# Perceiver kernel on one Trainium2 core: minima and token mixing on GpSimd, paired tokens in dilated attention, output by halves of the heads, and the last unit turned on TensorE

## The reference, cut to what matters

```python
# L0 token mixing (attn): Xn = layernorm(X) * gamma + beta
Q, K, V = split(Xn @ W_in + b_in)
K, V = rotary(K), rotary(V)
A = sum_over_tokens(K / |K| * V / |V|)
Y = ((0.5 * A + 0.5)[:, None, :] * Q) @ W_out + b_out
# L1 cross attention: 16 heads of 16, 4096 keys (both contexts), 8-bit steps
attn = softmax(q @ k.T)            # q, k rounded by head, v by column
attn = round(attn / s) * s         # s = max(attn) / 255
x += concat(attn @ v) @ Wp + bp
# L1 dilated attention: segments of 64 tokens, even heads take the even
# tokens, odd heads the odd ones; q = k = v = the gathered tokens
out = softmax(g @ g.T * hd ** -0.5) @ g
```

## Time and profile before

| | us |
|---|---|
| runs | 771.82, 774.67, 775.24 |
| profiled execution: its own time | 774.18 |
| its span, first to last instruction | 772.9 |
| PE busy | 673.9 (87%) |
| DVE busy | 587.5 (76%) |
| ACT busy | 373.3 (48%) |
| POOL busy | 124.6 (16%) |
| mean granted TensorE clock | 0.949 |

### The profile page before, as it was taken

How to read it: one execution, slowest core, us unless ns; L and a number is a source line. 1 busy time by engine, 2 the same in 40 slices (tenths; PEclk the granted TensorE clock), 3 DMA queues, 4 the chain that set the end, 5 groups by cost and what they waited for, 6 DMA issues and landing times. The chain is left out here.

```text
span 772.9 us, 12776 instructions
## 1 busy us (share of the span) xinstructions
PE 673.9 (87%) x4880; PEld 427.3 (55%) x4880; DVE 587.5 (76%) x1143; ACT 373.3 (48%) x581; POOL 124.6 (16%) x138
## 2 busy tenths in 40 slices
PE   5899999999999998997998999877897878778543
PEld 4456766666676675675665767633553434334231
DVE  3797867957866879787684787299989999999135
ACT  4453433343343343344332544137678987769411
POOL 3374234333433201000000000001000010000010
PEclk9999999999999998999999999989999999989755
DMA  9478967656665677964685747467788999779800
GB/s 300 103 144 157 189 130 124 130 117 127 119 124 123 144 142 195 206 138 91 137 177 112 150 100 143 86 180 152 146 146 145 202 173 147 152 129 165 151 1 7
DMA packets 334940, 108.24 MB, mean 140 GB/s; under 512 B 301464, under 2 KB 332320, under 8 KB 334624
## 3 DMA queue, kind: packets, MB, share of 16 engines
q1 hardware_dynamic: 334880, 107.43, 69.3%
HBM read 32.16 MB, written 0.26 MB: 42 GB/s over the span
## 5 line engine op out<-in xcount | busy, mean ns | idle before, releaser
L800 PE MATMUL psum<-c_nat,eT 128*128 128x256 f16 x1536 | 191.3, 276 | 0.0
L1455 ACT ACTIVATE cT<-psum,bias,q_scale 128x1024 f16<-128x1024 f32 x128 | 153.7, 1203 | 43.5 <-PE psum L1401 37.1
L1401 PE MATMUL psum<-kT,v_space 128*128 128x512 f16 x512 | 144.5, 390 | 34.1 <-DVE tops L1482 32.4
L774 PE MATMUL psum<-cT,qk 128*128 128x512 f16 x768 | 171.0, 379 | 1.2 <-ACT cT L711 1.1
L800 PEld LDWEIGHTS psum<-c_nat,eT 128*128 128x128 f16 x1536 | 152.3, 99 | 26.9 <-issue 0.6
L1482 DVE TENSOR_REDUCE tops<-psum 128x1 f32<-128x512 f32 x256 | 160.0, 682 | 1.6 <-PE psum L1401 1.4
L774 PEld LDWEIGHTS psum<-cT,qk 128*128 128x128 f16 x768 | 74.9, 98 | 86.0 <-ACT cT L711 1.3
L1401 PEld LDWEIGHTS psum<-kT,v_space 128*128 128x128 f16 x512 | 45.2, 98 | 108.1 <-DVE tops L1482 82.6
L924 DVE TENSOR_REDUCE neg_max<-psum 128x1 f32<-128x2048 f32 x32 | 73.3, 2290 | 31.3 <-PE psum L774 31.2
L912 DVE TENSOR_TENSOR e_lo<-e_all,e_hi 128x2048 f16<-128x2048 f32 x32 | 76.8, 2401 | 0.5 <-DMA eT<-e_lo 0.5
L438 POOL TENSOR_TENSOR rstd<-rstd,minus_half 128x1 f32<-128x1 f32 x12 | 9.5, 792 | 375.1 <-DVE rstd L433 375.1
(11 more groups left out here) (219 smaller groups left out, 740.9 us busy)
## 6 DMA issues: line engine op xcount, KB each, us to landing
wq_h<-in_L_xattn_Wq SPq DMA_DIRECT2D x32, 128.0 KB, 2.3
wk_h<-in_wkT SPq DMA_DIRECT2D x32, 128.0 KB, 2.2
wv_h<-in_L_xattn_Wv SPq DMA_DIRECT2D x32, 128.0 KB, 2.3
wo_h<-in_L_xattn_Wo SPq DMA_DIRECT2D x32, 128.0 KB, 2.2
mx_land<-in_mx_weights SPq DMA_DIRECT2D x8, 384.0 KB, 3.5
v_space<-in_ctx SPq DMA_DIRECT2D x4, 512.0 KB, 7.1
cT<-in_ctx SPq DMA_DIRECT2D x2, 1024.0 KB, 10.8
c_nat<-in_expert_wT SPq DMA_DIRECT2D x2, 1024.0 KB, 6.6
```

The costliest lines, as they stand in the source:

```text
L774: ins = pe.matmul(s_ps[:, n * 512:(n + 1) * 512], c.qk[:, u % 2, q_part, k, :], m.cT[:, b, c_part, 4 * n:4 * n + 4, k, :], start=(k, q_par ...
L800: ins = pe.matmul(u_ps, c.eT[:, v % 2, e_part, j, :], m.c_nat[:, v // H0, c_part, j, :], start=(j, e_part, c_part) == (0, 0, 0), stop=(j, ...
L1401: return pe.matmul(ps, m.qT[:, b, group, r, :], m.kT[:, group, at:at + BLK], start=True, stop=True)
L1455: act.activation(x.y[:, u % 2, q * CHUNK:(q + 1) * CHUNK], m.bank(3 + 2 * (q % 2), 2), ACT.Exp, bias=x.bias[:, u:u + 1], scale=m.q_scale[: ...
```

## The change

**Second stage.** `dve_attention` keeps the maxima alone. The smallest of eight goes to GpSimd (`pool_attention`): four `tensor_scalar` of one column, each as soon as two or three more maxima are there, the last with the factor q_scale, and a fifth for the constant. GpSimd's other work is woven into the same stream by slots.

**Token mixing.** For both batches, gamma, beta, the additions to x, the rotation, the product and the norms go from `dve_mix` to `pool_mix`. The two passes for 0.5·A + 0.5 and Q become one, and a factor 0.5 goes to ScalarE's copy. The slots of batch 0 stay; for batch 1 one is added behind `turn` and one behind `unit`.

**Output.** By halves of the heads. Heads 0 to 7 of batch 0 are woven in behind the queries of batch 1 (slots 43 to 46), those of batch 1 at slots 106 to 109. The values' scale no longer multiplies the result: GpSimd multiplies it into Wp's rows once (`wp1_scaled`), so two diagonals, one product and one copy of the first stage go.

**Dilated attention.** TensorE adds the tokens of a pair (product with the table `pair`); VectorE sets the groups apart from PSUM; scores, maximum, subtraction and exponential go by halves; two heads' exponentials are turned in one transpose of 128 columns, and four products of 64 columns take the place of eight of 32. Five tables come in one DMA.

**Last unit.** Its two DMA transposes go. TensorE turns eight blocks of 512 by products with the identity, VectorE copies seven, ScalarE one.

The core of the diff:

```diff
-MIX_WOVEN = "xT+plus qkv0 qkv1 qkv2 turn squares product unit a yT out"
+MIX_WOVEN = "xT+plus qkv0 qkv1 qkv2 turn turning squares product unit united a yT out"
-OUT_WOVEN = "gather yT out"
-DIL_WOVEN = "apply xT own s0 s1 nat t0+den t1 t2 t3 pv"
+OUT_WOVEN = ("gather0 yT0 out0", "gather1 yT1 out1")
+DIL_WOVEN = "apply xT own nat s0 s1+exp0 t0+exp1 t1+den pv"
...
+def pool_mix(pool, m, x, s, b, at):
...
+    pool.tensor_tensor(m_b, m_b, w["gamma"], ALU.mult).then_inc(sem, 1)
+    pool.wait_ge(sem, MIX_POOL["gamma"])
+    pool.tensor_tensor(m_b, m_b, w["beta"], ALU.add).then_inc(sem, 1)
...
+def pool_attention(pool, m, x, s, side):
...
+        for k in range(NB // 2):
+            top = [x.tops[:, u, n:n + 1] for n in range(2 * k + (k > 0), min(2 * k + 3, NB))]
+            side.upto(NC * u + k - ahead)
+            pool.wait_ge(s["q_max"], min(NB * u + 2 * k + 3, NB * (u + 1)))
+            if k > 0:
+                pool.wait_ge(s["q_steps"], NC * u + k)
+            if k == 0:
+                ins = pool.tensor_scalar(least, top[0], top[1], top[2], ALU.min, ALU.min)
+            elif k < NB // 2 - 1:
+                ins = pool.tensor_scalar(least, least, top[0], top[1], ALU.min, ALU.min)
+            else:
+                ins = pool.tensor_scalar(least, least, top[0], m.q_scale[:, b, h:h + 1], ALU.min, ALU.mult)
+            ins.then_inc(s["q_steps"], 1)
+        pool.wait_ge(s["q_steps"], NC * (u + 1))
+        pool.tensor_scalar(x.bias[:, u:u + 1], least, float(np.log(255.0 / N_UP)), None, ALU.add).then_inc(s["q_bias"], 1)
...
+    def turn(n):
...
+        pe.wait_ge(s["q_exp"], NC * (UNITS - 1) + n * BLK // CHUNK + 1)
+        if n >= 3:
+            pe.wait_ge(s["q_back_dve"], n - 2)
+        if n == 0:
+            pe.wait_ge(s["q_max"], NB * UNITS)
...
+            if u >= UNITS and q < 2:
+                for n in range(NB // 4 * (2 * (u - UNITS) + q), NB // 4 * (2 * (u - UNITS) + q + 1)):
+                    turn(n)
             if u > 1 and q < 2:
                 attend(u - 2, q)
...
+    for n in range(NB - 1):
+        dve.wait_ge(s["q_back"], n + 1)
...
+        back(dve.tensor_copy, x, m, n).then_inc(s["q_back_dve"], 1)
...
+def pe_output(pe, m, x, a, s, b, half, room, at):
+    sem, cols = s[f"at_pe{b}"], half_of(half, D)
+    yield at[f"gather{half}"]
+    yield from pe_leave(pe, room, at[f"gather{half}"], s[f"at_dve{b}"], AT_DVE[f"over_sum{half}"])
...
+    for k in range(KD):
+        ins = pe.matmul(room[1][:, k * OWN:(k + 1) * OWN], x.mine[:, k * P:(k + 1) * P], a.pair[:, 0:OWN], start=True,
+                        stop=True)
...
+    for n in range(PAIRS // 2):
+        pe.wait_ge(s[f"dil_act{b}"], DIL_ACT["t1" if n >= PAIRS // 4 else "t0"])
+        ins = pe.matmul(room[7][:, n * DIL * DW:(n + 1) * DIL * DW], x.scT[:, n, :], flat(x.nat[:, n]), start=True,
+                        stop=True)
```

More of the change, by code:

```diff
@@ L89 @@
 CONSTANTS = steps("zeros ones minus_half ident ident16 ident_fp16")
-V_SCALE_PE = steps("turned spread inverse")
-V_SCALE_DVE = steps("top clamp over diag0 diag1 idiag0 idiag1 scale inverse")
+V_SCALE_PE = steps("turned inverse")
+V_SCALE_DVE = steps("top clamp over diag0 diag1 inverse")
 MIX_PE = steps("xT q k v a yT out")
 MIX_ACT = steps("xT k_norm v_norm yT")
-MIX_DVE = steps("gamma beta plus_norm plus_bias q k v turn0 turn1 cos rotated product norms unit a y added")
+MIX_DVE = steps("q k v y added")
+MIX_POOL = steps("gamma beta plus_norm plus_bias turn0 turn1 cos rotated product norms root unit")
 EX_PE = steps("xT gate prod0 prod1 prod2 prod3 prod4 prod5 prod6 prod7 coefT bias")
@@ L100 @@
 QU_DVE = steps("biased scaled amax clamp inverse over up both0 both1")
[L101 to L106, removed]
+AT_PE = steps("yT0 out0 yT1 out1")
+AT_ACT = steps("yT0 yT1")
+AT_DVE = steps("total0 over_total0 over_sum0 added0 total1 over_total1 over_sum1 added1")
+DIL_PE = steps("xT own nat s0 s1 t0 t1 pv")
+DIL_ACT = steps("xT nat0 nat1 exp0 exp1 t0 t1")
+DIL_DVE = steps("parity apart0 apart1 s0 top0 less0 s1 top1 less1 den inv share over added")
 FF_PE = steps("aT g0 u0 g1 u1 g2 u2 g3 u3 mT0 mT1 out")
@@ L343, in __init__ @@
         self.bp1 = sb("bp1", [P, D])
-        self.mask = sb("mask", [P, OWN])
-        self.row_mask = sb("row_mask", [P, DIL])
+        self.sets = sb("sets", [P, SETS])
+        self.mask = self.sets[:, 0:OWN]
+        self.pair = self.sets[:, OWN:OWN + P]
+        self.row_mask = self.sets[:, OWN + P:OWN + P + DIL]
+        self.blocks = self.sets[:, OWN + P + DIL:SETS - DIL]
+        self.halves = self.sets[:, SETS - DIL:SETS]
 class AttentionTiles:
@@ L841, in pe_cross @@
         if u == H0 + 1:
[L842 to L845, removed]
+            pe.wait_ge(s["v_scale_dve"], V_SCALE_DVE["diag1"])
+            pe.matmul(kv_ps[:, 0:D], m.ones[:, :], g.diagonals[:, :], start=True, stop=True).then_inc(
+                s["v_scale_pe"], 1)
         if 0 <= v < UNITS:
@@ L1049, in dve_value_scales @@
     dve.wait_ge(sem, V_SCALE_DVE["over"])
[L1050 to L1053, removed]
+    for k in range(KD):
+        dve.tensor_scalar(g.diagonals[:, k * P:(k + 1) * P], m.ident[:, :], g.inverse[:, k:k + 1], 1.0 / N_UP,
+                          ALU.mult, ALU.mult).then_inc(sem, 1)
     dve.wait_ge(s["v_scale_pe"], V_SCALE_PE["inverse"])
-    dve.tensor_copy(m.v_scale[:, :], ps[:, D:2 * D]).then_inc(sem, 1)
     dve.wait_ge(s["scores"], H0)
@@ L1485, in dve_attention @@
[L1485 to L1496 removed]
+        least = x.least[:, u:u + 1]
```

380 lines of the change are left out of this document (208 added, 172 removed).

## The result

| | before | after |
|---|---|---|
| median of 4 runs, us | 774.94 (771.82 to 775.24) | 750.55 (746.82 to 751.36) |
| ratio, 95% interval | | 0.9685 (0.9644 to 0.9725) |
| profiled execution / its span, us | 774.18 / 772.9 | 750.32 / 749.0 |

The account below looks back on a forecast made before the run. TensorE was taken to bound the first attention, VectorE the second, before a serial tail. From 774.2 us, minus 12.0 (second attention), minus 8.0 (tail), plus 1.5 (first stage) gave 755.7 us, range 746 to 767.

Parts of the forecast that it names:

- Parts 1 to 3: Second attention: minimum, bias and batch 1's mixing leave VectorE, other work comes; 15.5 us off VectorE, 12.0 off the time.
- Part 4: Serial tail after the last exponential: turning, output and dilated attention gain 8.0 us together, from 5 to 10.
- (a): Tail, last exponential to division: TensorE turns the last unit instead of two DMA transposes; gain 1.6 us, 0 to 3.5.
- (b): Tail, output by the last eight heads: v_scale step goes, transposes, product and division are halved; gain 2.1 us.
- (c): Tail, dilated attention: new order with earlier start and eight product instructions instead of sixteen; gain 4.3 us, 3 to 5.5.
- Part 5: First stage: one product fewer, but batch 0's mixing on GpSimd delays TensorE; +1.5 us in all, -1 to +5.
- The term of the scales: First stage, line 844: one of two TensorE products goes and the wait before them shortens; -0.8 us.
- The term of beta: First stage: gamma and beta on GpSimd each wait for a VectorE step, so beta reaches TensorE later; +2.2 us.
- A: Second attention: DMA transposes or TensorE's hand-overs take over as bound, leaving 4 of 12 us; 763.7 us, chance 0.18.
- C: Second attention: GpSimd's chain of minima becomes the bound, ScalarE's first exponential waiting for the bias; 792 us, chance 0.04.
- D: Whole kernel: minima net 0, tail gives 5 us, TensorE's first-stage stalls cost 5; 774 us, chance 0.03.
- B: Whole kernel: second attention's relief comes whole at 16 us, tail gives 9, first stage 0; 749 us, chance 0.12.

Follow-up runs that it names:

- experiment 2: Kernel after with batch 1's token mixing back on VectorE, in the new slots, GpSimd keeping the powers: median 751.10 us, ratio 0.9688.
- experiment 4: Kernel after with batch 0's token mixing (first stage) back on VectorE, batch 1's staying on GpSimd: median 748.24 us, ratio 0.9624.
- experiment 6's first kernel: Kernel after with the last unit's exponentials turned by two DMA transposes again instead of TensorE: 751.26 us, ratio 0.9697.
- experiment 7: Kernel after with first-stage slots later: two transposes, 745.46 us; batch 0's mixing also on VectorE, 746.72, or 750.13 with experts' transposes at (24, 0), gate at (24, 1).

## Why the prediction came out as it did

The time came 5 us under the forecast, and that it lies in the range is in part luck: one part had the wrong sign, and one sum was added up wrongly.

**Parts 1 to 3**, the second attention: 12.0 predicted, 11.5 in the profile, 10.7 between the averages. The terms as they stand don't give 12.0: of 15.5 us, 11.2 lie in the woven units, 80% of that is 9.0, and with 2.8 from the free units and 1.0 less for the two waits it makes 10.8. The step of GpSimd was right (0.37 for 0.35), and so was the spare time: 1.1 left by the forecast, 1.2 measured. The next limit was not where I put it: free units reach 4.78, not 4.95, though their DMA share stays at 1.14. What gave less were the woven units. What mixing gave of its 4.5 us isn't told (experiment 2).

**Part 4**: (a) 1.6 predicted, 1.5 in the profile, at half clock; (b) output 4.62 to 2.86, 1.8 for 2.1; (c) dilated 4.3 predicted, 5.8 in the profiles; the medians' 4.3 has too wide an interval to decide. The products at half clock take 1.81, close to the 1.9 of the forecast, so what it missed lies in the steps before them. Together 9.0 for 8.0.

**Part 5 is the step that failed**, by its sign: +1.5 predicted, -4.8 between the two profiles, some -3 between the averages of two and of seven. The term of the scales was right (-0.8 forecast, some 1.0 measured). The term of beta was right for the move alone (+2.2 forecast, 1.8 of pause by experiment 4), but the pause grew by 1.0 only, since VectorE reached the mixing 0.9 us sooner. Put at nothing were TensorE's other pauses: the one before `u_sb` is gone (0.9 and 1.1 before), the one before the experts' transposes is 3.4 instead of 3.9 and 4.3, the one before the fourth product 2.0 to 2.2 instead of 2.6 and 2.7. For the first the trace shows the shorter transposes; the other two stay that short with the mixing back on VectorE (3.5 and 2.1), so the move isn't their cause, which I did not follow further. The rest of the 4.8 is chance in the clock: before, three stretches of half clock fall in these units, 17.1 us in all, in its second profile 10.2, as in after; 3.4 us of half clock take 1.7 (unit 26 to 27 with identical code: 18.23 us without such a stretch, 19.95 with one of 3.4, in experiment 6's first kernel).

**Rivals.** A is excluded by the free units and by the stage's 11.5 us, C by the spare time, D by the total. B's 749 is nearer to the result than my 755.7, but not by its reasons: the relief came at 11.5, not 16.

The rule on VectorE and GpSimd (the Trainium skill, SBUF — State Buffer, section Who interferes with whom) gave the right sign for batch 0's mixing. It calls the lock exclusive for the whole instruction; by an estimate from that rule and the durations alone, a pair would take 0.95 + 0.67 = 1.62 us, and the pairs above start 1.40 apart (302.31, 303.71), so the two overlap a little here.

## What to carry to other kernels

Small steps behind a bound engine's work can go to an idle engine as long as the consumer's spare time covers the longer chain: measure that time by a delay, since here 1.9 us more cost 1.5 us by the medians, no more than chance, and 4.2 us cost 29. Where steps move to a slower engine, move the slots of their consumers too: one such slot and one at a pause that was there before gave 5.1 us together, a fifth of this whole change; a slot moved past a step that waits for a landing took 3.4 of it back (experiment 7, 750.13 against 746.72). Where TensorE is the bound, cut the stage at TensorE's own instructions: another engine's marks moved by 0.9 us and showed gains that weren't there. And before crediting a gain to the edit, compare the landing times of the DMAs that it left alone.

## What the runs showed that I had not expected

- The same DMA transposes took 1.94 or 1.63 us on SyncE and landed after 4.4 or 3.7 us in two builds that place their tiles differently.
- A pause of TensorE of 2 to 5 us was followed by 3.4 or 6.8 us of half clock, or by none: the same code gave each of these in different executions, and 3.4 us of half clock cost 1.7.
- The tail from the division on takes 35.9 us at half clock for all but 1.0 us of it (experiment 7), 35.4 with 6.8 us at full clock in it (after).
- TensorE's pauses come back within 0.2 us in seven executions of the same code (4.5 to 4.7 before the mixing's transposes), the half clock behind them doesn't.
